# Two gated blocks on one core: the shared block's down products turned around in fp32r parts

## What is computed

```python
x = L0_attn_hidden_states                                    # 1024 tokens x 256
xn = _layernorm(x, axis=-1)
s = _L0_attn_ref(xn, Wq, Wk, Wv, Wo)                         # 16 heads of 16, 4 key heads, softmax
gate, up = jnp.split(jnp.einsum('bsh,oh->bso', xn, w_gate_up), 2, axis=-1)
h = jax.nn.silu(gate) * up                                   # 1024 wide
g = _silu(jnp.einsum('bsi,hi->bsh', h, w_down))              # the down product, 256 wide
x = x + s * g
# layer 1: linear attention, and 8 experts of which each token takes the best
```

## Time and profile before

| what | value |
|---|---|
| timed runs | median 336.7 us of 3 (336.23 to 338.54) |
| the profiled execution | 335.74 us, of which the span from first to last instruction is 333.5 |
| mean granted clock of PE | 0.993 |
| busy, share of the span | PE 95%, DVE 67%, ACT 48%, POOL 20% |

### The profile page before, as it was taken

One profiled execution on the slowest core, in us unless ns is written; L12 is line 12 of the kernel. 1 busy time (PEld: TensorE's weight loads), 2 busy tenths in 40 slices (PEclk: granted clock), 3 DMA queues, 4 the chain that ended last, 5 costly groups with the idle time before them and its releaser, 6 DMA issues.

```text
span 333.5 us, 4912 instructions
## 1 busy us (share of the span) xinstructions
PE 317.5 (95%) x1646; PEld 189.5 (57%) x1646; DVE 223.9 (67%) x489; ACT 161.4 (48%) x299; POOL 66.9 (20%) x90
## 2 busy tenths in 40 slices
PE   8889999999999999999999999999999999999990
PEld 8655564455555545465455456546654677665650
DVE  3978968695566667868976772129899666454972
ACT  1794457566768455544384455532406622233230
POOL 5009633700030000000000002200321441116132
PEclk9999999999999999999999999999999999999997
DMA  7910073091280650400000005106944896034721
GB/s 221 422 41 0 0 151 108 4 221 37 65 192 3 130 129 9 118 2 2 0 3 1 0 2 206 48 2 249 375 166 115 317 428 264 16 129 145 249 92 36
DMA packets 19867, 39.19 MB, mean 118 GB/s; under 512 B 1698, under 2 KB 15235, under 8 KB 18688
## 3 DMA queue, kind: packets, MB, share of 16 engines
q1 hardware_dynamic: 18448, 35.69, 33.6%
q0 software_dynamic: 1392, 3.15, 2.7%
HBM read 34.02 MB, written 15.22 MB: 148 GB/s over the span
## 4 chain that ended last, share of the span: by engine, by line
PE 83%; DVE 11%; issue 2%; DMA 1%; ACT 1%; POOL 0%; SPq 0%; DVEq 0%; POOLq 0%
PE ps L1816 10%; PE ps L1759 9%; PE ps L1727 9%; PE ps L1829 8%; PE ps L1749 8%; PE ps L1871 6%; PE ps L1887 6%; PE ps L1899 6%; PE ps L1628 4%; PE ps L1564 3%; DVE nmax L1292 3%; PE ps L1661 3%; PE ps L1936 2%; PE ps L1607 2%; PE ps L1861 1%
## 5 line engine op out<-in xcount | busy, mean ns | idle before, releaser
L1292 DVE TENSOR_REDUCE nmax<-ps 128x1 f32<-128x512 f32 x128 | 85.2, 687 | 36.4 <-PE ps L1727 35.3
L1019 ACT ACTIVATE shared<-ps 128x512 f32<-128x512 f32 x128 | 73.8, 594 | 43.1 <-PE ps L1749 42.1
L1727 PE MATMUL ps<-experts 96*128 96x512 bf16 x128 | 47.8, 384 | 2.4 <-DVE experts L1299 1.1
L1749 PE MATMUL ps<-experts 99*128 99x512 bf16 x128 | 48.3, 383 | 0.0
L1829 PE MATMUL ps<-shared,experts 128*128 128x256 f32 x128 | 37.7, 386 | 0.2 <-DVE gated L1337 0.2
L1759 PE MATMUL ps<-shared,experts 128*32 128x512 f32 x256 | 34.1, 605 | 0.3 <-ACT shared L1019 0.3
L1727 PEld LDWEIGHTS ps<-experts 96*128 96x128 bf16 x128 | 12.4, 98 | 37.4 <-DVE nmax L1292 20.3
L1829 PEld LDWEIGHTS ps<-shared,experts 128*128 128x128 f32 x128 | 23.2, 191 | 8.7 <-issue 2.5
L1027 ACT ACTIVATE experts<-ps 96x1024 bf16<-96x1024 bf16 x18 | 18.3, 1021 | 9.8 <-PE ps L1661 9.6
L1628 PE MATMUL ps<-late_weights,xnT 128*128 128x512 f32 (+1 forms) x64 | 22.5, 492 | 0.4 <-DVE shared L1199 0.4
L1871 PE MATMUL ps<-experts,shared 128*128 x88 | 21.0, 382 | 0.8 <-ACT shared L1094 0.8
(11 more groups left out here) (236 smaller groups left out, 541.1 us busy)
## 6 DMA issues: line engine op xcount, KB each, us to landing
experts<-in_experts SPq DMA_DIRECT2D x8, 1536.0 KB, 12.0
slot_rows<-in_empty SPq DMA_DIRECT2D x4, 2080.0 KB, 11.5
shared<-in_wgu SPq DMA_DIRECT2D x2, 1024.0 KB, 9.1
shared<-in_wdn SPq DMA_DIRECT2D x1, 1024.0 KB, 11.4
expert_results<-in_empty SPq DMA_DIRECT2D x1, 1024.0 KB, 6.9
token_rows<-x SPq DMA_DIRECT2D x1, 1024.0 KB, 15.4
token_rows<-gx SPq DMA_DIRECT2D x1, 1024.0 KB, 4.5
shared<-expert_results SPq DMA_DIRECT2D x4, 256.0 KB, 5.6
```

Source lines behind the costliest of these rows:

```text
L1019: nc.scalar.activation(probs[:, n % 2, hh, :], ps[:, 2 + hh % 2, :], ACT.Exp, scale=float(HD) ** -0.5).then_inc(s["exp_done"], 1)
L1292: nc.vector.tensor_reduce(nmax[:, 4 * t + hh:4 * t + hh + 1], ps[:, m % 2, :], AX, ALU.max, negate=True).then_inc(s["max_done"], 1)
L1727: nc.tensor.matmul(ps[:, m % 2, :], qs[0:KS, b, GR * g + hh, P * t:P * t + P], ks[0:KS, b, g, :], start=True, stop=True).then_inc(s["score ...
L1749: nc.tensor.matmul(ps[:, 2 + hh % 2, :], ks[0:KM, b, g, P * t:P * t + P], qs[0:KM, b, GR * g + hh, :], start=True, stop=True).then_inc(s[" ...
```

## The change

1. The down products are turned around: `down_high`/`down_low` (128 inner rows x 128 of the 256 outputs) are the weights, `h_high`/`h_low` (512 tokens wide) the moving operand, three fp32r products per i and per half c of the outputs, banks 6 and 7 for the halves. `fill` holds them as (i, both halves) and `put` inserts them, as it does gate and up, in pairs.
2. The results lie with outputs on partitions. Tanh and product are done there 512 wide (into `gated`), and `back` transposes both halves (two `back` items per batch, each two token tiles x two halves of the outputs, so four 128x128 transposes; 16 in all), and ACT copies each item's bank to `gx`.
3. Parts of h: `h_parts` is a rounding on ACT (into the room of the x parts, four in use: `PARTS`) and a subtraction on POOL. It is placed right behind a `prob`, and a down item is not placed before `LAG` = 3 further `prob`s have been (`ready`); the same holds for `back` behind the last down.
4. Parts of the down weights: `round_down` (ACT, 128x1024 for each of two halves) at (4, 2) and (6, 3), `lower_down` on POOL in place of `wdn`. The first down product and that with i = 4 of the first batch wait for `w_low_ready` 5 and 6.
5. POOL follows the plan: `lower_rows(1)`, `router_c` and `scatter(0)` stand where the plan has them.
6. The pace ends 8 heads before the end; the costs of down and back in `Clock` are new.
7. Small: the 0.5 tile is filled by POOL, two semaphores are joined in `table_stored`, the bias add of layer 1 is waited for by DVE itself at once.

```diff
+PARTS = 4
+LAG = 3
-    PE = {..., "down": .43, ...}
+    PE = {..., "down": .69, "back": .6, ...}
...
+        elif kind == "h_parts":
+            self.other("act", .6, ("h_high", item[1]))
+            self.other("pool", 1.25, ("h_low", item[1]), self.done[("h_high", item[1])])
+        elif kind == "round_down":
+            self.other("act", 1.1, ("rounded",))
...
-        for j in range(TB):
-            fill += [("down", b * TB + j, i) for i in range(NI)]
-    cost = {"gate": 3, "up": 3, "down": 2}
+        fill += [("down", 2 * b + c, i) for i in range(NI) for c in range(2)]
+        fill += [("back", 2 * b + c, 0) for c in range(2)]
+    cost = {"gate": 3, "up": 3, "down": 3, "back": 3}
...
+    due(4, 2, ("round_down", 0))
+    due(6, 3, ("round_down", 1))
...
+    def ready(f):
+        if f[0] == "down":
+            return probs[0] - placed.get(NI * (f[1] // 2) + f[2], probs[0]) >= LAG
+        return f[0] != "back" or probs[0] - placed["down"] >= LAG
...
-        while fill and (spent < pace - SLACK or ...):
-            clock.run(fill[0])
-            emit()
+        while fill and ready(fill[0]) and (spent < pace - SLACK or ...):
+            for _ in range({"back": 1, "down": 2 - fill[0][1] % 2}.get(fill[0][0], 2 - fill[0][2] % 2)):
+                clock.run(fill[0])
+                emit()
...
+        if coming and item[0] == "prob" and (item[1] % TB, item[2]) not in ((2, 1), (2, 2), (2, 3), (3, 0)):
+            part()
...
-            pace = start + (total - start) * (GR * n + hh + 1) / (GR * STEPS)
+            pace = start + (total - start) * (GR * n + hh + 1) / (GR * STEPS - 8)
...
+            def lower_down(half):
+                pool.wait_ge(s["w_high_ready"], 5 + half)
+                i0 = NI // 2 * half
+                w = wdn[:, i0:i0 + NI // 2, :].rearrange("p i n -> p (i n)")
+                high = (down_high1 if half else down_high0).bitcast(F32)
+                at_ = 2 * KD * INTER + D * i0
+                nc.gpsimd.tensor_tensor(w_low_words[:, at_:at_ + NI // 2 * D], w, high, ALU.subtract).then_inc(s["w_low_ready"], 1)
+            def lower_h(c):
+                pool.wait_ge(s["h_high_ready"], c + 1)
+                b, i = divmod(c, NI)
+                nc.gpsimd.tensor_tensor(h_low(i), hT[:, i, :], h_high(b, i).bitcast(F32), ALU.subtract).then_inc(s["h_low_ready"], 1)
...
+                elif kind == "round_down":
+                    act.wait_ge(s["parts_done"], B + 1)
+                    act.wait_ge(s["down_wo_loaded"], 32)
+                    i0 = NI // 2 * it[1]
+                    nc.scalar.activation(down_high1 if it[1] else down_high0, wdn[:, i0:i0 + NI // 2, :].rearrange("p i n -> p (i n)"),
+                                         ACT.Copy).then_inc(s["w_high_ready"], 1)
+                elif kind == "h_parts":
+                    b, i = divmod(it[1], NI)
+                    if i < PARTS:
+                        act.wait_ge(s["up_ready"], NI * (b + 1))
+                    else:
+                        act.wait_ge(s["down_ready"], 2 * (NI * b + i - PARTS + 1))
...
-            nc.vector.memset(tanh_g[:, 0, 0:P], 0.5).then_inc(s["halves_ready"], 1)
+            nc.gpsimd.memset(tanh_g[:, 0, 0:P], 0.5).then_inc(s["vone"], 1)
...
                 elif kind == "down":
-                    ins = nc.tensor.matmul(ps[:, bk, 0:D], hT[:, i, P * (j % TB):P * (j % TB) + P], wdn[:, i, :],
-                                           start=i == 0, stop=i == NI - 1)
+                    if j == 0 and i in (0, NI // 2):
+                        pe.wait_ge(s["w_low_ready"], 5 + i // (NI // 2))
+                    if c == 0:
+                        pe.wait_ge(s["h_low_ready"], NI * b + i + 1)
+                    w_parts = [w[:, P * c:P * c + P] for w in (down_high(i), down_low(i))]
+                    h_parts = [h_high(b, i), h_low(i)]
+                    for n_, (w_, h_) in enumerate(((0, 0), (0, 1), (1, 0))):
+                        ins = nc.tensor.matmul(ps[:, bk, :], w_parts[w_], h_parts[h_], start=i == 0 and n_ == 0, stop=i == NI - 1 and n_ == 2)
+                    ins.then_inc(s["down_ready"], 1)
+                elif kind == "back":
+                    for a in range(2):
+                        for c in range(2):
+                            at_ = P * (2 * half + a)
+                            last = nc.tensor.transpose(ps[:, bk, P * (2 * a + c):P * (2 * a + c) + P], gated[:, c, at_:at_ + P], ident)
```

More of the change, by code:

```diff
@@ L124 @@
 FIRST_STACKS = 5
+PARTS = 4
+LAG = 3
 SLACK, AHEAD = 2, 16
 class Clock:
-    PE = {"prob": .22, "score": .22, "values": .9, "stack_T": .45, "gate": .65, "up": .65, "down": .43, "heads_norm": .43, "max_rows": .22,
+    PE = {"prob": .22, "score": .22, "values": .9, "stack_T": .45, "gate": .65, "up": .65, "down": .69, "back": .6, "heads_norm": .43, "max_rows": .22,
           "attn_T": .43, "wo": 1.7, "wo_half": 1.7, "rows_T": .43, "logits": 3.4, "counts": .4}
@@ L271, in attention_plan, with part @@
     plan = []
+    clock = Clock()
+    coming = []
+    placed = {}
+    probs = [0]
+    def part():
+        clock.run(coming[0])
+        placed[coming[0][1]] = probs[0]
+        plan.append(coming.pop(0))
+    def ready(f):
+        if f[0] == "down":
+            return probs[0] - placed.get(NI * (f[1] // 2) + f[2], probs[0]) >= LAG
+        return f[0] != "back" or probs[0] - placed["down"] >= LAG
     def emit():
@@ L277, in emit @@
         spent += cost[f[0]]
+        if f[0] == "down":
+            while coming and coming[0][1] <= NI * (f[1] // 2) + f[2]:
+                part()
         plan.append(f)
@@ L280, in emit @@
             plan.append(("gated", f[1]) if f[2] == 0 else ("hidden", f[1]))
-        return plan[-1]
+            if f[2] and f[1] % NI == NI - 1:
+                coming.extend(("h_parts", f[1] - NI + 1 + i) for i in range(PARTS))
+        if f[0] == "down":
+            placed["down"] = probs[0]
+        if f[0] == "down" and f[1] % 2 and f[2] < NI - PARTS:
+            coming.append(("h_parts", NI * (f[1] // 2) + f[2] + PARTS))
     def early(n):
@@ L838, in scatter @@
                         in_=xn[:, j, :], in_offset=None).then_inc(s["scattered"], 16)
-            scatter(0)
+            for it in plan:
+                kind = it[0]
+                if kind == "round_down":
+                    lower_down(it[1])
+                elif kind == "round" and it[2] == KD - 1:
+                    lower_rows(1)
+                elif kind == "h_parts":
+                    lower_h(it[1])
+                elif kind == "logits":
+                    pool.wait_ge(s["router_mean"], 1)
+                    mean = small[:, 1, 0:E].rearrange("p (o e) -> p o e", o=1)
+                    nc.gpsimd.tensor_tensor(router_c[:], router[:], mean.to_broadcast([P, KD, E]), ALU.subtract).then_inc(s["router_centred"], 1)
+                elif kind == "place":
+                    scatter(0)
             scatter(1)
```

121 lines of the change are left out of this document (69 added, 52 removed).

## The result

The changed kernel takes **351.68 us** (median of 4 runs, 351.06 to 351.81), the kernel before 337.6 in the same comparison (336.23 to 338.54): a ratio of 1.0434, 95% interval 1.0404 to 1.0464. It is slower, as forecast, but by 14 us where 6.6 were forecast (5.6 by the sum and 1.0 for the clock), and outside the range of 335.5 to 346.0. The profiled execution took 351.06 us with a span of 349.3.

What follows compares the result with a forecast made beforehand. TensorE, busy 317.5 of 333.5 us, was taken as the bound. Terms -4.5 - 0.8 + 4.7 + 4.1 + 2.0 + 0.1 = +5.6 on 335.7 gave 341.3, with +1.0 for the clock 342.3 us; range 335.5 to 346.0.

Steps and rivals of the forecast that it cites:

- term 7: TensorE's granted clock behind the two new waits: one fall with 2.5 us of slow work, +1.0 us, ends 0 and +2.8.
- term 5: Attention steps and the last steps: pieces in pairs and filling out early leave TensorE gaps, +1.0 and +1.0 us.
- terms 1 and 2: TensorE: cheaper turned down products, -4.5 us; eight pieces in step 0 where four stood, filling holes, -0.8 us.
- Terms 3 and 4: First down piece and down piece 4: TensorE waits for POOL's low parts of the weights, +4.7 and +4.1 us.
- Term 6: Added work hidden on other engines: some +14 us on ACT, 25 us on POOL; small edits 0.1 us together.
- Rival A: At both down-weight waits: the waits are covered, 332.7 us as the middle; chance 0.13.
- Rival D: Whole kernel: clock falls behind both waits and coarse filling reaches its far end, 346.1 us; chance 0.18.
- Rival B: At the two down-weight waits: only one comes, the other hidden by unseen holds, 336.9 us; chance 0.15.

Runs made afterwards that it cites:

- f1: The changed kernel with the down weights' high and low parts made during step 0 and the preparation, pairs and pace kept: 342.02 us, ratio 1.0141.
- e3: The kernel before with only the change's coarse filling (pairs, pace ending 8 heads before the end), fp32 down products kept: 338.59 us, ratio 1.0045.
- f3: The changed kernel with early weights' parts, single pieces, the old pace, and filling moved to beside the router's logits: 336.92 us, ratio 1.001.
- a1: The changed kernel with single pieces and the pace of the kernel before, weights' parts still rounded where the change has them: 336.52 us, ratio 0.9969.
- b1: a1 with gate 15 moved from steps 22 and 23 to right ahead of and behind the router's logits: 335.72 us, ratio 0.997.
- e4: The changed kernel with single pieces, old pace, down pieces held 8 heads after their weights' rounding, second half rounded at (5,0): 335.79 us, ratio 0.9953.
- e2: The changed kernel with 20 and 12 extra bf16 products, results unused, ahead of the two waits: 348.5 us, ratio 1.0349.
- a2: The changed kernel with pairs kept but the pace of the kernel before: 342.27 us, ratio 1.015.
- d1: a1 with the second half of the down weights rounded at head (9,0) in place of (6,3): 338.84 us, ratio 1.008.
- f2: f1 with every piece placed alone and the pace of the kernel before: 336.52 us, ratio 1.0006.
- a3: The changed kernel with single pieces but its own pace: 338.92 us, ratio 1.0066.

## Why the prediction was right in sign and wrong in size

The step that failed most is term 7, the price of the clock: +1.0 us forecast, 5.9 measured. Then come the gaps of coarser filling (term 5, +2.0 forecast, 4.2 measured) and the saving of terms 1 and 2 (-5.3 forecast, -3.8 measured). Behind them stands a wrong idea of what makes the waits.

**Terms 3 and 4, the two waits: right.** 5.11 and 4.04 us, forecast 4.7 and 4.1, both for POOL's line 894 and by the order given. What the forecast did not say is that the first wait hides 2.4 us of others (f1), so that removing it gives back less than its length.

**Term 7, the clock: wrong, the largest miss.** "I count one fall, with 2.5 us of slow work behind the pause: +1.0 us", with 2.8 as the far end. There were three, with 11.8 us of slow work, 5.9 lost. Two steps failed. The granted clock fell 3.3 us behind the start of the first pause, but it did not rise soon after TensorE went back to work: 5.0 us of busy time followed in it at the first place, and 3.4 at each of the others. And behind the second pause it fell only 1.07 us after work had begun again (at 100.22). The third fall stands behind no long wait; I had no term for it, since I looked only at pauses longer than 2.9 us. I also priced slow work at four tenths of its length, from warm-up rows; the piece rows behind the first wait pass in 0.43 us against 0.23, nearly a half.
The Trainium skill (TensorE: Matmul & The Clock Gate, "HAM oscillation — how this bites in real kernels") says that waits for data make the next block start cold, every time in its example, and that this costs half of the slow time. By that rule both falls would have come, and at nearly the half that the rows here show (0.43 us against 0.23): for these two waits the trace agrees, and the rule should have had more weight than the one fall that I counted. That section tells nothing of the third, which stands behind products of 8 columns and not behind a pause.

**Term 5, coarser filling: right in place, too small.** Forecast +2.0 with a far end of +4. Idle time outside the two waits grew by 4.2 us: 1.4 in steps 20 to 23, 2.6 from step 28 on, and the rest in small gaps. e3 has the coarse filling alone on the kernel before at +2.15; its profile shows 1.7 of idle time and 1.7 of slow work more, and 0.6 of other work less.

**Terms 1 and 2, the products: saving put too high.** Forecast -4.5 and -0.8. In the profile of f3, which has no slow stretch, the distances between starts over all pieces, down products, their transposes, `prob` and `score` sum to 133.6 us, before to 136.8: -3.2, a little beyond my near end of -3.4. The old down products were as I had them, 29.1 us by these distances against my 28.8. The turned ones with their transposes take 28.6, and `prob` and `score` beside them 2.6 less: 26.0 us where I had 24.3. Step 0 saved its 0.3 us of idle time and no more. The rest of all versions with the turned products in the table lies 2.4 to 3.8 us below that of before.

**Term 6, what is hidden: right.** POOL's busy time grew by 25.3 us, as counted, and ACT's by 8.9 where I had 14.

**The step that I missed altogether** is in the rivals. I took "where the pieces stand" as given by the turned products, and put the waits down to the lag. The pairs and the faster pace are edits of their own, and they, not the turned products, put the first down pair one head behind the rounding: a1 takes both out and loses nothing against the kernel before. So terms 3, 4, 5 and 7, together +11.8 us in the forecast, all belong to these two edits, which are worth 15.2 us (351.7 - 336.5). Rival A (waits covered, 332.7) is a1 in kind, 3.8 us too low; its condition was not ACT or POOL being ahead, but single pieces. That the waits would come was right by the order as given; what they come of was not asked.

**By the sum**, from TensorE's first product to its last: forecast +6.6, came +15.5. Of the 8.9 us between them the clock has 4.9, the gaps of coarse filling 2.2, the products and step 0 1.5, and the waits 0.35. Rival D (346.1), with both falls and the far end of the filling, came nearest; it lacked the third fall and the half. Rival B fell with the second wait.

**What the turned products are worth.** a1 against before is 0.3% (0.9943 to 0.9995), b1 the same (0.9947 to 0.9993), e4 0.5% (0.9923 to 0.9983), all within what I called no change. TensorE does about 2.5 us less; idle time takes 2.1 us of it back: 1.8 more from step 28 on, where before down products were still there to place, 0.7 more in steps 4 to 7, and 0.4 less elsewhere.

## What to carry to other kernels

Where a change both replaces an operation and alters how it is placed, cost the two apart: here the operation is worth 0.3 to 0.5 per cent and the placing cost over four, in the main because it brought readers forward onto weights whose parts are made by another engine in its own order. A distance counted in heads from one producer (h) does not protect against a second one (the weights) whose place is fixed. And a pause of TensorE can cost more than its length: those of 4.0 and 5.1 us here brought a slow stretch each, 3.2 us for both by e2; one of 2.3 us brought none in the execution profiled.

## What the runs showed of the hardware that I had not expected

**Some runs hold a slow stretch that the profile lacks.** The runs of one kernel fall into groups that follow their mean granted clock: of 29 runs of the kernel before, 20 took 336.2 to 336.9 us at a mean of 0.992 to 0.994, and 9 took 338.0 to 338.8 at 0.987 to 0.989; of ten runs of a1, four took 334.6 to 335.0 and six 336.5 to 337.2 at the same two levels. A profile of a1 with one slow stretch of 3.42 us (177.38 to 180.80) belongs to the group of 0.987 to 0.989. So one such stretch costs about 2 us, by estimate, and the kernel before seems to have one too in three runs of ten, though its profile shows none; that is read from the means alone. Group against group, a1 is 1.4 to 1.6 us faster than before.

**It also comes without a pause.** In nine of fourteen profiles a slow stretch begins 2.1 to 3.5 us behind the first row of the logits. Six of the nine (a1, a2, d1, e3, e4, f2) have no gap of TensorE at all in steps 20 to 23. In e2 and f1 one begins 2.6 and 3.3 us ahead of the logits, behind the gap of 1.30 us. It is absent in b1 and f3, which have pieces next to them, but in a3 and the kernel before too. That pieces beside the logits make it rarer is supported (3 of 12 runs of b1 have the lower mean clock, 6 of 10 of a1; f3, with 4 of 12, against 5 of 12 in f2, says little); that the logits are its only cause is not shown.

**DVE's copies take longer beside POOL's subtractions.** DVE's copy of 128x1024 bf16 takes 0.42 us with POOL at rest, as all three do in the kernel before, and more beside POOL's subtractions:

```profile
68.09 0.42 DVE L1405 COPY experts<-experts 128x1024 bf16<-128x1024 bf16 x1
...
72.24 0.99 DVE L1405 COPY experts<-experts 128x1024 bf16<-128x1024 bf16 x1
...
74.34 1.52 DVE L1405 COPY experts<-experts 128x1024 bf16<-128x1024 bf16 x1
```

Between 71.67 and 78.07 POOL never rests; the third copy starts with its third subtraction (74.31) and ends 0.28 us behind it. The Trainium skill (SBUF — State Buffer, "Who interferes with whom") says that such copies can use a pair of ports that POOL uses too, and that whoever has it holds it for the whole instruction while the other stands still; the rows agree. Here this lay under the first wait. In f1, where that wait is gone, the third copy takes 1.52 us too and ends at 76.16; the stack's transposes, which wait for it, start at 76.26 behind 1.69 us of idle time. So about 1.1 us of that is likely this, an estimate (1.52 - 0.42); it was not tried by itself.
